# Local transformer stream: the Newton step of the inverse lengths moved to GpSimd, and the order of work rewritten on every engine

## What is computed

```
for i in range(6):                                    # DEPTH
    # attention, 16 heads of 64 channels, windows of 32 tokens
    q, k, v = split(shift(x) @ Wqkv[i])
    q = q / max(|q|, 1e-12) * q_scale[i];  k likewise   # lengths over 64 channels
    q, k = rotary(q), rotary(k)
    sim = q @ [k of the window before, k of this window]^T * 8, masked
    x = x + (softmax(sim) @ v) @ Wo[i]
    # feed-forward
    xn = layernorm(shift(x))
    a, g = split(xn @ W1[i] + b1[i])
    x = x + (a * gelu(g)) @ W2[i] + b2[i]
```

## Time and profile before

| | |
|---|---|
| median of 3 runs | 4416.31 us (4412.99 to 4423.09) |
| the profiled execution: its own time | 4419.39 us |
| its span in the profile | 4417.6 us |
| busy, share of the span | PE 88%, DVE 78%, ACT 72%, POOL 61% |
| mean granted clock of PE | 0.94 |

### The profile page before, as it was taken

One profiled execution on the slowest core, in us unless ns is written; L12 is line 12 of the kernel. 1 busy time (PEld: TensorE's weight loads), 2 busy tenths in 40 slices (PEclk: granted clock), 3 DMA queues, 4 the chain that ended last, 5 costly groups with the idle time before them and its releaser, 6 DMA issues. The chain is left out here.

```text
span 4417.6 us, 164417 instructions
## 1 busy us (share of the span) xinstructions
PE 3899.8 (88%) x64144; PEld 2853.1 (65%) x64144; DVE 3447.6 (78%) x6675; ACT 3176.4 (72%) x10347; POOL 2673.5 (61%) x2507
## 2 busy tenths in 40 slices
PE   7966968999999999999954896899999999999996
PEld 3423437777777777777734664777777777777773
DVE  1132129999999999999943664999999999999994
ACT  3343337888888888888841433788888888888884
POOL 1110127777777777777710332777777777877772
PEclk8987989999999999999975987999999999999997
DMA  1101113333333333333310000333333333333341
GB/s 58 57 15 44 57 47 105 115 103 119 100 116 103 106 112 108 114 97 109 117 29 0 1 0 33 103 112 104 119 99 116 104 108 112 103 117 98 106 119 37
DMA packets 549303, 377.81 MB, mean 86 GB/s; under 512 B 32576, under 2 KB 533056, under 8 KB 546240
## 3 DMA queue, kind: packets, MB, share of 16 engines
q1 hardware_dynamic: 548560, 367.57, 27.6%
HBM read 265.37 MB, written 102.11 MB: 83 GB/s over the span
## 5 line engine op out<-in xcount | busy, mean ns | idle before, releaser
L1266 POOL TENSOR_TENSOR lt_t<-lt_t 128x512 f32<-128x512 f32 x768 | 973.5, 1289 | 567.8 <-DVE lt_t L1100 567.8
L1002 ACT ACTIVATE lt_pb<-lt_pb,lt_mx 128x64 f32<-128x64 f32 x3072 | 1023.5, 346 | 0.0
L1272 POOL TENSOR_TENSOR lt_t<-lt_t,lt_rn 128x512 f32<-128x512 f32 x768 | 810.8, 1076 | 118.4 <-DVE lt_rn L1128 117.1
L49 PE MATMUL ps<-lt_wh,lt_xh 128*128 128x512 f32 (+1 forms) x1536 | 581.8, 379 | 148.9 <-DVE lt_t L1100 87.6
L1002 ACT ACTIVATION_READ_ACCUMULATOR lt_pb<-lt_pb,lt_mx 128x1 f32 x3072 | 610.2, 199 | 0.0
L984 ACT ACTIVATE lt_qkT<-ps 128x512 f32<-128x512 f32 x768 | 459.0, 598 | 197.2 <-PE ps L804 196.8
L1111 DVE TENSOR_REDUCE lt_ss<-lt_sq 128x8 f32<-128x512 f32 x768 | 518.7, 675 | 14.5 <-ACT lt_sq L979 9.9
L1100 DVE TENSOR_TENSOR lt_t<-ps,lt_tab 128x512 f32<-128x512 f32 x768 | 522.9, 681 | 2.9
L51 PE MATMUL ps<-lt_wh,lt_xl 128*128 128x512 f32 (+1 forms) x1536 | 523.7, 341 | 0.0
L1106 DVE TENSOR_TENSOR lt_t<-ps,lt_tab 128x512 f32<-128x512 f32 x768 | 521.6, 679 | 1.6 <-PE ps L804 0.3
L50 PE MATMUL ps<-lt_wl,lt_xh 128*128 128x512 f32 (+1 forms) x1536 | 522.8, 340 | 0.0
(11 more groups left out here) (196 smaller groups left out, 7989.3 us busy)
## 6 DMA issues: line engine op xcount, KB each, us to landing
lt_vw<-v_scratch SPq DMA_DIRECT2D x768, 256.0 KB, 3.7
v_scratch<-lt_vv SPq DMA_DIRECT2D x384, 256.0 KB, 2.1
lt_wraw<-in_lt_wqkv SPq DMA_DIRECT2D x56, 384.0 KB, 5.6
moe_cbc<-comb_scratch SPq DMA_DIRECT2D x16, 1024.0 KB, 6.7
moe_w<-in_moe_w SPq DMA_DIRECT2D x32, 256.0 KB, 2.8
lt_wo<-in_lt_wo SPq DMA_DIRECT2D x48, 128.0 KB, 3.7
lt_w<-in_lt_w SPq DMA_DIRECT2D x12, 341.0 KB, 4.2
lt_w<-in_lt_w SPq DMA_DIRECT2D x12, 192.0 KB, 3.3
```

What stands on the lines that cost most here:

```text
L49: nc.tensor.matmul(out, lh, rh, start=start, stop=False)
L1002: ins = nc.scalar.activation(p, p, ACT.Exp, bias=mx[:, par, c:c + 1], accum_out=sm[:, par, c:c + 1])
L1266: nc.gpsimd.tensor_tensor(o, o, t2[:, t, :], ALU.add).then_inc(padd[t], 1)
L1272: nc.gpsimd.tensor_tensor(o, o, rn[:, u[1] % 2, 8 * t:8 * t + 8].unsqueeze(2).to_broadcast([P, 8, DH]), ALU.mult).then_inc(qkd[t], 1)
```

## The change

Five things change, and nothing in what is computed. (1) `newton` moves from DVE to POOL, where it is four operations on 128x16 numbers in place of three, each waiting for the one before it. (2) The order of pieces within a slot is another on PE, ACT, DVE, POOL and SP. (3) Some pieces are done for another unit than before: lengths, floor and first guess one slot later, `turn(u, 1)` before `turn(u, 0)` of the next unit, `normalise_qk(u, 1)` and `add_turned(u, 1)` one slot later, `values` and `take_values` for u2 in place of u1, `turn_weights` for u5 in place of u4. (4) Feed-forward pieces sit at other distances. (5) The waits follow the new order. `next_batch` itself is not touched.

```diff
@@ tensor: turn, values @@
                     if t == 0:
-                        upto(pe, vE, u)
+                        upto(pe, vE, back(u, 1))
...
                 def values(u):
                     j, half = u[1] % GJ, batch(u) % 2
-                    upto(pe, tE[1], back(u, 1))
+                    upto(pe, tE[1], u)
@@ tensor: slot @@
+                    if u5:
+                        turn_weights(u5)
...
                     if u0:
                         project(u0, 0)
                         project(u0, 1)
...
                     if u2:
-                        turn(u2, 0)
...
+                        turn(u2, 1)
                     if u5:
                         weigh(u5)
...
                     if u2:
-                        turn(u2, 1)
-                    if u4:
-                        turn_weights(u4)
+                        values(u2)
+                        scores(u2)
                     if u5:
                         merge(u5)
-                    if u2:
-                        scores(u2)
...
                     if u1:
-                        values(u1)
...
+                        turn(u1, 0)
@@ vector @@
                 def floor(u):
                     upto(dve, ssd[0], u)
                     upto(dve, ssd[1], u)
+                    upto(dve, rnd, back(u, 2))
...
-                def newton(u):
@@ gpsimd @@
+                def newton(u):
+                    par = u[1] % 2
+                    upto(pool, y0d, u)
+                    nc.gpsimd.tensor_tensor(ya[:, par, :], y0[:, par, :], y0[:, par, :], ALU.mult).then_inc(newt, 1)
+                    upto(pool, newt, u, 1, 3)
+                    nc.gpsimd.tensor_tensor(yb[:, par, :], ya[:, par, :], vm[:, par, :], ALU.mult).then_inc(newt, 1)
+                    upto(pool, newt, u, 2, 3)
+                    nc.gpsimd.tensor_tensor(ya[:, par, :], yb[:, par, :], res["three"][:, :], ALU.subtract).then_inc(newt, 1)
+                    upto(pool, newt, u, 3, 3)
+                    nc.gpsimd.tensor_tensor(rn[:, par, :], ya[:, par, :], y0[:, par, :], ALU.mult).then_inc(rnd, 1)
...
                 def slot(L, s):
-                    u0, u1, u3 = unit(L, s), unit(L, s - 1), unit(L, s - 3)
-                    c = chunk(L, s, 16)
-                    if c:
-                        low(c)
+                    u0, u1, u2, u4 = unit(L, s), unit(L, s - 1), unit(L, s - 2), unit(L, s - 4)
                     if s == 15 and running(L):
                         low_up(pool, L)
+                    if u2:
+                        normalise_qk(u2, 1)
+                    if u0:
+                        next_batch(u0)
                     if u1:
+                        add_turned(u1, 1)
+                    if u4:
+                        normalise_weights(u4)
+                    c = chunk(L, s, 16)
+                    if c:
+                        low(c)
+                    if u1:
+                        newton(u1)
                         normalise_qk(u1, 0)
-                        normalise_qk(u1, 1)
                     if u0:
                         add_turned(u0, 0)
-                        add_turned(u0, 1)
-                    if u3:
-                        normalise_weights(u3)
-                    if u0:
-                        next_batch(u0)
```

More of the change, by code:

```diff
@@ L773, in slot @@
                 def slot(L, s):
-                    u1 = unit(L, s - 1)
+                    u2 = unit(L, s - 2)
                     if not isinstance(L, int) or L < DEPTH:
                         reload(L, s)
-                    if u1:
-                        spread(u1)
-                stream(sp, slot, 1)
+                    if u2:
+                        spread(u2)
+                stream(sp, slot, 2)
                 for j in range(GJ):
@@ L926, in slot @@
                 def slot(L, s):
-                    u0, u1, u2, u4, u5 = unit(L, s), unit(L, s - 1), unit(L, s - 2), unit(L, s - 4), unit(L, s - 5)
-                    c = chunk(L, s, 17)
+                    u0, u1, u2, u5 = unit(L, s), unit(L, s - 1), unit(L, s - 2), unit(L, s - 5)
+                    c = chunk(L, s, 23)
                     if c:
-                        gate(c, 1)
+                        down(c)
+                    if u5:
+                        turn_weights(u5)
+                    c = chunk(L, s, 18)
+                    if c:
+                        linear(c, 0)
                     c = chunk(L, s, 13)
@@ L936, in slot @@
                         project(u0, 1)
-                    c = chunk(L, s, 17)
-                    if c:
-                        gate(c, 2)
-                    c = chunk(L, s, 23)
-                    if c:
-                        down(c)
-                    if u2:
-                        turn(u2, 0)
-                    c = chunk(L, s, 17)
-                    if c:
-                        linear(c, 0)
                     c = chunk(L, s, 18)
@@ L950, in slot @@
                         linear(c, 1)
+                    if u2:
+                        turn(u2, 1)
                     if u5:
                         weigh(u5)
+                    c = chunk(L, s, 17)
+                    if c:
+                        gate(c, 1)
+                    c = chunk(L, s, 17)
+                    if c:
+                        gate(c, 0)
+                    c = chunk(L, s, 21)
+                    if c:
+                        linear(c, 2)
                     c = chunk(L, s, 14)
@@ L1046, in slot @@
                         high(c)
-                    c = chunk(L, s, 17)
-                    if c:
-                        gelus(c)
-                    if s == 15 and running(L):
-                        high_up(act, L)
-                    if u0:
-                        square_of(u0, 0)
                     c = chunk(L, s, 14)
@@ L1192, in slot @@
                 def slot(L, s):
-                    u0, u1, u2, u3, u5 = unit(L, s), unit(L, s - 1), unit(L, s - 2), unit(L, s - 3), unit(L, s - 5)
-                    if u3:
-                        maxima(u3)
-                    if u1:
-                        newton(u1)
-                    c = chunk(L, s, 17)
+                    u0, u1, u2, u3, u4, u5 = unit(L, s), unit(L, s - 1), unit(L, s - 2), unit(L, s - 3), unit(L, s - 4), unit(L, s - 5)
+                    c = chunk(L, s, 18)
                     if c:
                         product(c, 0)
+                    if u1:
+                        lengths(u1, 0)
+                    c = chunk(L, s, 13)
+                    if c:
+                        deviation(c)
                     c = chunk(L, s, 15)
@@ L1232, in slot @@
                         update(c)
+                    if u0:
+                        cosine(u0, 0)
+                        sine(u0, 0)
+                    if u2:
+                        take_values(u2)
+                    if u0:
+                        cosine(u0, 1)
+                        sine(u0, 1)
+                    c = chunk(L, s, 21)
+                    if c:
+                        product(c, 2)
+                    if u5 and u5[1] % GJ == GJ - 1:
+                        update_x(u5)
+                    if u2:
+                        mask_scores(u2)
                 dve.wait_ge(fvlld, 16)
@@ L1691, in program @@
         tiny = sb("tiny", [P, 16])
+        three = sb("three", [P, 16])
         rank = sb("rank", [P, TILES, EXPERTS])
@@ L1713, in _ @@
                 nc.gpsimd.memset(tiny[:, :], 1e-24)
+                nc.gpsimd.memset(three[:, :], 3.0)
                 nc.gpsimd.memset(ln1024[:, :], float(10.0 * np.log(2.0)))
```

93 lines of the change are left out of this document (37 added, 56 removed).

## The result

| | before | after |
|---|---|---|
| median, us | 4417.15 (4412.99 to 4423.09, 4 runs) | 4943.24 (4939.73 to 4944.88, 4 runs) |
| ratio to before | | 1.1191, 95% interval 1.1177 to 1.1205 |
| the profiled execution; its span | 4419.39; 4417.6 | 4944.04; 4942.2 |

The change made the kernel 11.9% slower. The direction was forecast, the size was not: 4943 us lies 228 us above the forecast and 103 above its range.

A forecast was written before the change was run, and what follows sets the result against it. DVE bounds the kernel before (97% busy), PE close behind. With PE's new stall a slot takes 8.74 us: 4417.6 + 215 + 86 for the clock = 4719, given as 4715 us, 6.8% slower, range 4525 to 4840.

The forecast's parts named there:

- DVE relieved: Moving newton takes some 1.4 us a slot off DVE's 7.9, so it needs 6.5 and no longer bounds.
- Newton's price: Newton's four linked operations on POOL cost 1.16 us a slot, between 0.76 and 1.9.
- Rival B: Newton costs 1.9 us on POOL and makes POOL's way the longer one: about 4838 us, chance 0.08.
- The new stall: Every fourth slot next_batch waits on POOL for values; the 6.17 us chain behind it leaves PE standing 4.4 us.
- The clock: PE's clock drops to half behind the long stalls, costing 86 us in all.
- three in four of the 96 stalls: The share of PE's stalls taken to lose clock, at 1.2 us each, 86 us together.
- Costed at nothing: ACT has more time than before: ACT, 87% busy at 8.18 us a slot, gets more time, so nothing was added for it.
- PE's own work: PE's slot without feed-forward taken as 6.4 us; with feed-forward 60.4 us for eight slots, 7.55 a slot.
- The high end: Half a microsecond more at floor per stall, 96 clock losses of 1.6 us, newton at 1.5: 4867, stopped at 4840.
- A, the clock holds: The stall is there but PE's clock stays steady: 4632 us, chance 0.28.
- C, no stall: PE doesn't stand still and its 7.55 us a slot sets the pace: faster, 4175 us, chance 0.11.
- D: Gain and loss cancel, with stalls of 2.5 us and a steady clock: 4416 us, chance 0.03.

The follow-up runs named there:

- e3: The kernel before with only newton moved to POOL, as four operations ahead of normalise_qk, with floor's wait to match: 4338 us, ratio 0.9814.
- e1: The changed kernel with next_batch put back at the end of POOL's slot: 4579 us, ratio 1.0358 to the kernel before.
- e8: The changed kernel with zero-weight matmuls (8 or 5) added into merge's sums on PE during the stall: 4807 us, ratio 1.0890 to the kernel before.
- e4: The changed kernel with low_group on POOL moved one slot later, after normalise_weights(u4): 4872 us, ratio 1.1022 to the kernel before.
- e11: The changed kernel with merge(u5) ahead of scores(u2) on PE and nothing else: 4905 us, ratio 1.1109 to the kernel before.
- e12: The changed kernel with zero-weight matmuls in PE's wait, low_group one slot later and merge ahead of scores, next_batch still second: 4712 us, ratio 1.0676.
- e7: The changed kernel with next_batch last in POOL's slot, low_group one slot later and merge ahead of scores: 4396 us, ratio 0.9959 to the kernel before.
- e5: The changed kernel with next_batch last in POOL's slot and low_group one slot later: 4460 us, ratio 1.0100 to the kernel before.

## Why the prediction was right or wrong

**DVE relieved, right, but by less.** The forecast took 1.4 us a slot off DVE; the three operations of newton in the trace of before are 251.4 + 179.2 + 97.1 = 527.7 us, 1.37 a slot. DVE's busy time fell from 7.9 us a slot to 6.9 (1226.32/1700 of 9.58), not to 6.5; 0.2 of the difference is floor, which now takes 445 ns in the mean in place of 248. This changed nothing in the sum, since DVE bounds in neither case. By e3 the relief is worth 78 us by itself.

**Newton's price, right.** 1.16 us were worked out from two wider operations, 1.19 were measured (1455.07 to 1456.26). The grouped row of one of the four:

```profile
L1269 POOL TENSOR_TENSOR lt_rn<-lt_ya,lt_y 128x16 f32<-128x16 f32 x384 | 85.1, 222 | 30.0
```

Rival B falls with it.

**The new stall, right, in place, cause and size.** The chain was forecast at 6.17 us and is 6.1. PE's wait was forecast at 4.4 us, or 3.7 where gate 2 stands in the stall, 389 us in all; it is 4.29 and 2.2 to 3.6, and the 96 waits are 356 us. That 96 x 4.4 = 422 lies near the 429.0 of the table is chance, since 73 us of that row lie in other slots. e1 shows that the stall is the main loss.

**The clock, right in kind, too small.** e8 gives some 136 us, the sum had 86. Two steps were mis-sized. One is "three in four of the 96 stalls": in the trace of after the granted clock stands at 0.50 for part of the 12 us behind the cast in 91 of the 96 (in before in 5 of 96). The other is "3.4 us" of slow time behind a wait. That length came from a wait of 2 us; behind a stall of after, PE's timeline has slow matmuls from 1495.6 to 1500.6, 5.0 us:

```profile
1495.60:1500.60 5.00, 5.00 (x16) 4.32 (x17) 1.78 (x3) 2.21 (x8) 3.34 (x3) 0.50 0.24 48
```

PE's timeline of that place:

```profile
1495.53 1.12 PE L806 MATMUL ps<-ident,lt_t 128*128 128x128 f32 x4 [2.73 <-POOL lt_t L1275]
1496.44 1.06 PE L846 MATMUL ps<-ident,lt_pb 128*128 128x128 f32 x4
1497.15 0.78 PE L49 MATMUL ps<-lt_rh,lt_w1h 128*128 128x512 f32 x1
...
1501.13 0.40 PE L49 MATMUL ps<-lt_rh,lt_w1h 128*128 128x512 f32 x1
```

Nine wide matmuls take 3.98 us from 1497.15 to 1501.13, and 2.1 at 0.23 each; turn and turn_weights take 1.62 us together, and 0.93 in the earlier trace rows. So this stall lost 2.6 us to the clock, one of the dearer ones. The Trainium skill's pattern (TensorE: Matmul & The Clock Gate, "HAM oscillation — how this bites in real kernels"), a loss in every round, is nearer to these 91 of 96 than the forecast's three in four: it gave 29 us more, and 50 were missing.

**"Costed at nothing: ACT has more time than before", wrong.** This is the step that failed outright. ACT did have time, but the argument went by its busy share and not by the order of its list. high_group is last there, behind the copy of the slot's last turn, and low_group on POOL waits for it (103.2 us, 46 times) ahead of rows that PE needs: 22 of PE's waits at turn 0 lie right behind. Moving it one slot later gave 72 us (e4). The sum did hold 3.4 us a layer, 41 us, for low_group's own work on POOL; no run tells how much of the 72 that already covers.

**PE's stops in scores, missing in the sum.** 39 us (e11). Before has 12 of these stops, 3.5 us in all, so a reading of before could not price them; that weigh and scores had come closer together could be read off the order. They end with the arrival of instructions, a limit that no term held.

**PE's own work, too small by 0.14 us a slot.** The rows gave 6.5 us for a slot without feed-forward, and the forecast took 6.4, "since a turn that needn't wait is a little shorter". It isn't so: two such slots of after, without a wait, from weigh to weigh:

```profile
1352.27 1.14 PE L864 MATMUL ps<-lt_pT,lt_vw 64*64 64x32 f32 x64
...
1358.77 1.14 PE L864 MATMUL ps<-lt_pT,lt_vw 64*64 64x32 f32 x64
...
1365.28 1.14 PE L864 MATMUL ps<-lt_pT,lt_vw 64*64 64x32 f32 x64
```

The trace of after has 123 of them, with a median of 6.51 us, that of e12 117, with 6.67; against 6.4 that is 8 x 0.27 = 2.2 us in eight slots of e12. The earlier trace rows had a warning: 1392.74/1470 of 8.18 are 7.75 us a slot, 0.20 above the 7.55 of the sum. A single part was off the other way and takes 1.1 of the 2.2 us back: mean and variance cost 0.56 us and not 1.1, as the start of values behind the variance at 1462.57 shows:

```profile
1462.57 1.13 PE L890 MATMUL ps<-lt_sqf,avg 128*128 128x512 f32 x2
1463.13 0.69 PE L49 MATMUL ps<-lt_wh,lt_xh 128*128 128x256 f32 x1
```

**The account.** The forecast is 4632 + 83 us of clock (86, less 3 for the median). Measured were 4632 + 80 (e12) + 232 (e12 against after) = 4944. So of the 228 us some 80 are in PE's work and an untraced rest, and 149 in the three losses beyond what the sum had for the clock.

**The range and the rivals.** The high end took a floor held up by POOL as the further mishap. It is held up, 445 ns in the mean in place of 248, but no run here prices that. What went wrong was elsewhere, in two stalls of a kind that had no term at all. A, the clock holds, is refuted by e8. C, no stall, stood at 4175 us. With the stall out of the way it was 4579 (e1), and with the two other repairs 4396 (e7), so PE's pace was never the 7.55 us a slot of that rival; D falls with it. Rival C's condition (a stall under 2.5 us) was rightly judged unmet.

## What to carry to other kernels

When an order is rewritten, take each wait and ask where in the same slot the row it waits for stands, on every engine, also the ones with time to spare: two of the four losses here were a row of POOL that waits, ahead of work that PE needs soon, for a row late in another engine's slot. Add the clock to each stall of some microseconds, and check a pace read from one slot against the busy time of the view that covers the whole. And try the parts of a change one by one: the move of newton was worth 1.9% by itself, and the new order around it, even with all repairs found here, stays 58 us behind the old order with newton moved (e7 against e3).

## What the runs showed of the hardware that was not expected

PE can stand for up to 2.3 us inside a run of 64 small matmul passes with no semaphore to wait for. All 157 such stops in the traces of after, e5 and e7 end 1.1 to 1.8 us behind a 16 KB transfer of instructions, and merge's four passes of 256 columns between two such runs take them from 79.6 to 11.3 us. Matmuls with zero weights, added into sums in progress, kept the granted clock over the stream at 0.99 where the waits alone had brought it to 0.92, and made the kernel 2.8% faster though they add work. A tensor_tensor of 16 columns takes 0.22 us on POOL, 0.30 from start to start where each needs the one before; the same on DVE beside a busy POOL took 0.47 and 0.66 us in the mean.
